# Moving the key and value projection behind a step's transposes in a paged-attention kernel

## The chip, the cores and the metric

The kernel runs on one core of a Trainium2 chip. TensorE multiplies and transposes, VectorE and ScalarE read its results out of PSUM, GpSimd does some elementwise work and issues the gathers, SyncE issues the other transfers. The metric is the device time of one execution in microseconds; the median of three runs of the kernel before is 1195.59 us (1194.82 to 1195.92).

## The reference, cut to what matters

Two layers with residual connections. The first is attention with 32 query heads, 8 key and value heads, 8 sequences of 128 tokens and a cache of 512 keys per sequence, gathered by pages:

```python
q, k, v = x @ Wq.T, x @ Wk.T, x @ Wv.T          # x: (8, 128, 512); 32, 8 and 8 heads of 128
q, k = rope(rmsnorm(q) * wq), rope(rmsnorm(k) * wk)
k_all, v_all = concat(cache[block_table], new)   # 512 cached keys and 128 new ones
p = softmax(where(valid, q @ k_all.T / sqrt(128), -1e30))
x = x + (p @ v_all) @ Wo.T
```

The second layer adds a 512x512 product and two of eight low-rank experts per token, chosen by logits. All is float32.

## The kernel before

The attention is cut into 64 groups: one key head (with its four query heads) and one sequence each. Float32 products are made of three matmuls each: every operand is split into a high part (a copy rounded to the fast format, made by ScalarE) and a low part (the rest, by subtraction on VectorE), and hi*hi, hi*lo and lo*hi are added up in PSUM (`three_passes`, lines 280 to 282). Helper `low` on line 664 does all of the subtractions, so many of VectorE's rows have that line.

One step `s` of a software pipeline, for s from -2 to 64, works on four groups at once: the attention of group s, the output product of group s-1, the transposes of queries and keys of group g1 = s+1, and the projections of group g2 = s+2. Each engine has its own function `step` and goes through its instructions strictly in that written order; semaphores join the engines. There is no planner.

TensorE's order in a step is: scores of heads 0 and 1 (line 1011), the output O of s-1, scores 2, transposes T0 of head 0's probabilities (line 1034), the query projection Q, scores 3, T1, the output projection Y, T2, the queries' transpose QT (line 1102, four 128x128 pieces), the cached keys' transpose KTC (line 1019, four), the key and value projection KV (12 matmuls, lines 280 to 282), the new keys' transpose KTN (line 1113, one), T3, and the transposes TN of the new keys' probabilities (line 1119, four). Then the next step's scores.

Scores have two PSUM buffers of their own (`ps_s`). All of the other results share four PSUM banks (`ps_w`) in turn, by their place in a fixed list:

```python
UNITS = ["O", "T0", "Q", "T1", "Y", "T2", "QT", "KTC", "KV", "KTN", "T3", "TN"]
```

A unit's bank is its place modulo 4, and `wait_bank` waits for the engine that last read the unit four places ahead. KTN waits for VectorE's split of T2, T3 for that of the queries (QT), TN for that of the cached keys (KTC), KV for the addition of Y, and the next step's O for ScalarE's copy of KV. The scores of the next step wait for the splits of queries, cached keys and new keys.

ScalarE goes through: copy and square of the projected keys and values at the start of a step, exponentials and normalisations of the heads, copies of T0 to T2, QT and KTC, then pieces of the next head's weights (`w_split`, `wo_split`), then KTN, T3 and TN. VectorE follows with the low parts in the order T2, QT, KTC, KTN, T3, TN; its `rowmax` (line 727) opens a step. In the steps -1 to 4 both split one more block of x at the end (`split_x`). In steps 62 and 63 there is no projection left; in some of its places four 128x128 pieces of the first layer's result y are transposed (`turn_x`, line 965). SyncE's `fetch_x` waits for KV and loads x again for four steps on.

Of the kernel before, what the change touches and what calls it, by code (L numbers as in the profile page):

```python
# [13 lines left out]
ACT = mybir.ActivationFunctionType  # L14
# [4 lines left out]
S = 128  # L19
# [6 lines left out]
L = PSIZE * NPP  # L26
KEYS = L + S
# [66 lines left out]
def attention_lora(nc, xT, x, wqkv, wo, kv, normw, kpos, consts, ints, w1, wB, out):  # L94
    with ExitStack() as ctx:
        def sb(name, shape, dt=F32):
            return ctx.enter_context(nc.sbuf_tensor(name, shape, dt))

        def sem(name):
            return ctx.enter_context(nc.semaphore(name))  # L100
# [24 lines left out]
        kt_hi, kt_lo = sb("kt_hi", [P, KEYS], F32R), sb("kt_lo", [P, KEYS], F32R)  # L125
# [77 lines left out]
        pe_q, pe_kv, pe_qt, pe_ktc, pe_ktn = sem("pe_q"), sem("pe_kv"), sem("pe_qt"), sem("pe_ktc"), sem("pe_ktn")  # L203
# [7 lines left out]
        a_qt, a_ktc, a_ktn, a_pt, a_norm, a_o = sem("a_qt"), sem("a_ktc"), sem("a_ktn"), sem("a_pt"), sem("a_norm"), sem("a_o")  # L211
# [18 lines left out]
        def has(g):  # L230

            return 0 <= g < G

        def wait(eng, s, g, per=1, nth=None):

            count = g * per + (per if nth is None else nth)
            if g >= 0:
                eng.wait_ge(s, count)

        def wait_kv(eng, g):  # L240

            eng.wait_ge(s_kv[g % 2], 64 * (g // 2 + 1))

        def bank(unit):
            return ps_w[:, UNITS.index(unit) % NBANK, :]
# [212 lines left out]
        def _(act):  # L458
# [62 lines left out]
            def step(s):  # L521
                g1, g2 = s + 1, s + 2

                def exps(h):

                    wait(act, d_max, s, 4, h + 1)
                    nc.scalar.activation(ps[:, h, :], ps[:, h, :], ACT.Exp, bias=negmax[:, s % 2, h:h + 1], scale=-1.0,  # L527
                                         accum_out=rowsum[:, s % 2, h:h + 1]).then_inc(a_exp, 1)

                def norm(h):  # L530

                    wait(act, d_recip, s, 4, h + 1)
                    nc.scalar.activation(ps[:, h, :], ps[:, h, :], ACT.Copy, scale=recip[:, s % 2, h:h + 1]).then_inc(a_norm, 1)  # L533

                def probs(h):

                    wait(act, pe_t, s, 4, h + 1)
                    nc.scalar.activation(pt_hi[:, 0:CT, h, :], bank(f"T{h}").rearrange("p (t q) -> p t q", t=CT),  # L538
                                         ACT.Copy).then_inc(a_pt, 1)

                def cached_keys():
                    wait(act, pe_ktc, g1)
                    nc.scalar.activation(kt_hi[:, 0:L], bank("KTC"), ACT.Copy).then_inc(a_ktc, 1)

                if has(g1):
                    wait(act, pe_kv, g1)
                    wait(act, p_v, g1 - 2, 2)
                    nc.scalar.activation(raw[:, g1 % 2, QW:WW], bank("KV")[:, 0:2 * D], ACT.Copy).then_inc(a_kv, 1)
                    wait(act, a_kv, g1)
                    wait(act, a_q, g1)  # L550
                    wait(act, d_m2, g1 - 1)
                    wait(act, p_m1, g1 - 1)
                    if s == -1:
                        act.wait_ge(d_wlo, KC)
                    nc.scalar.activation(u[:].rearrange("p h d -> p (h d)"), raw[:, g1 % 2, 0:QW + D], ACT.Square).then_inc(a_sq, 1)
                if s == -1:
                    sines()
                if has(s):
                    exps(0)
                    norm(0)  # L560
                    exps(1)
                    norm(1)
                if s == G:
                    expert_products(0)
                if has(s - 1):
                    wait(act, pe_o, s - 1)
                    wait(act, pe_y, s - 2)
                    nc.scalar.activation(o_hi[:], bank("O"), ACT.Copy).then_inc(a_o, 1)
                if s == G:

                    act.wait_ge(pe_s, 4 * G)
                    expert_products(1)
                    expert_products(2)
                if has(s):
                    probs(0)

                    wait_kv(act, s)
                    wait(act, a_kv, s)
                    wait(act, pe_o, s - 1)
                    nc.scalar.activation(v_hi[:, 0:CT, :], kv_raw[:, s % 2, :, D:2 * D], ACT.Copy).then_inc(a_vhi, 1)  # L580
                    nc.scalar.activation(v_hi[:, CT, :], raw[:, s % 2, QW + D:WW], ACT.Copy).then_inc(a_vhi, 1)
                    exps(2)
                    norm(2)
                if has(g2):
                    wait(act, pe_q, g2)
                    wait(act, d_u, g2 - 2)
                    if g2 == 1:
                        act.wait_ge(d_mask, B)
                    nc.scalar.activation(raw[:, g2 % 2, 0:QW], bank("Q"), ACT.Copy).then_inc(a_q, 1)
                turn_x(s, "Q")  # L590
                if has(s):
                    probs(1)
                    exps(3)
                    norm(3)
                    probs(2)
                if s == -1:
                    cached_keys()
                if has(g1):
                    wait(act, pe_qt, g1)
                    nc.scalar.activation(qt_hi[:], bank("QT"), ACT.Copy).then_inc(a_qt, 1)  # L600
                    if s != -1:
                        cached_keys()
                for n in W_AT.get(s, ()):
                    w_split(n)
                for n in WO_AT.get(s, ()):
                    wo_split(n)
                if has(g1):
                    wait(act, pe_ktn, g1)
                    nc.scalar.activation(kt_hi[:, L:KEYS], bank("KTN")[:, 0:S], ACT.Copy).then_inc(a_ktn, 1)
                for unit in ("QT", "KTC", "KV", "KTN"):  # L610
                    turn_x(s, unit)
                if has(s):
                    probs(3)
                    wait(act, pe_tn, s)
                    nc.scalar.activation(pt_hi[:, CT, :, :].rearrange("p h q -> p (h q)"), bank("TN"), ACT.Copy).then_inc(a_pt, 1)
                if s < 0:
                    first_wo_split(2 * (s + 2))
                    first_wo_split(2 * (s + 2) + 1)
                if 2 <= s + 3 < B:
                    split_x(s + 3)  # L620
# [41 lines left out]
        def _(dve):  # L662
            def low(out_ap, full, hi):
                return nc.vector.tensor_tensor(out_ap, full, hi.bitcast(F32), ALU.subtract)  # L664
# [52 lines left out]
            def step(s):  # L717
                g1, b = s + 1, s % B
# [93 lines left out]
                if has(g1):  # L812
# [3 lines left out]
                        cached_keys()  # L816
                    wait(dve, a_ktn, g1)
                    low(kt_lo[:, L:KEYS], bank("KTN")[:, 0:S], kt_hi[:, L:KEYS]).then_inc(d_ktn, 1)
                for unit in ("QT", "KTC", "KV", "KTN"):
                    turn_x(s, unit)  # L820
                if has(s):
                    probs(3)
                    wait(dve, a_pt, s, 5)
                    low(pt_lo[:, CT, :, :].rearrange("p h q -> p (h q)"), bank("TN"),
                        pt_hi[:, CT, :, :].rearrange("p h q -> p (h q)")).then_inc(d_pt, 1)
                if s < 0:
                    first_wo_split(2 * (s + 2))
                    first_wo_split(2 * (s + 2) + 1)
# [127 lines left out]
        def _(pe):  # L956
            def turn_x(s, unit):

                c = turned(s, unit)
                if c is None:  # L960
                    return
                wait(pe, d_y, G - B + c)
                wait_bank(pe, s, unit)
                for k in range(KC):
                    last = nc.tensor.transpose(bank(unit)[:, k * S:(k + 1) * S], y[:, c, k * P:(k + 1) * P], ident)
                last.then_inc(pe_xt, 1)
# [30 lines left out]
            def step(s):  # L997
                g1, g2 = s + 1, s + 2
# [106 lines left out]
                        turn_cached_keys()  # L1105
                turn_x(s, "QT")
                turn_x(s, "KTC")
                if has(g2) and s != -1:
                    project_keys_values()
                turn_x(s, "KV")  # L1110
                if has(g1):
                    wait_bank(pe, s, "KTN")
                    nc.tensor.transpose(bank("KTN")[:, 0:S], rot[:, REP, :], ident).then_inc(pe_ktn, 1)
# [1 line left out]
                if has(s):  # L1115
                    turn_probs(3)
                    wait_bank(pe, s, "TN")
                    for h in range(REP):
                        last = nc.tensor.transpose(bank("TN")[:, h * S:(h + 1) * S], ps[:, h, L:KEYS], ident)  # L1119
                    last.then_inc(pe_tn, 1)  # L1120

            for s in range(-2, G + 1):
                if s == -1:
# [97 lines left out]
```

## Time and profile before

| | |
|---|---|
| median of three runs | 1195.59 us |
| profiled execution | 1195.48 us |
| its span | 1193.7 us |
| TensorE matmul busy | 1155.7 us |
| TensorE weight load busy | 1025.5 us |
| ScalarE busy | 938.9 us |
| VectorE busy | 928.4 us |
| GpSimd busy | 768.2 us |

The span runs from the first to the last instruction. Busy times of TensorE are those of pipelined instructions whose ends are modelled, so the starts of its weight loads are the surest marks of where it stands. A wait that is put down to "issue" has no releaser that the profile names.

### The profile page before, as it was taken

To read this page: it belongs to the slowest core of one execution; us is meant where nothing else is said; L and a number is where in the kernel's file an instruction comes from. 1 tells how busy PE (TensorE), PEld (TensorE's weight loads), DVE (VectorE), ACT (ScalarE), POOL (GpSimd) and SP (SyncE) were. 2 spreads that over 40 slices of the span, in tenths; PEclk is the share of its full clock that TensorE was granted. 3 is DMA by queue.
4 is the path that set the end of the run, shared out by engine and by line. 5 is a ranking of instruction groups with operands and counts; after the bars stand their busy time and mean duration, and the time that the engine had idled before them with its cause. 6 is when DMAs were issued, how large, how long until landed. Compare 5 with 4: busy or idle time off the path is not lost.

```text
span 1193.7 us, 20774 instructions
## 1 busy us (share of the span) xinstructions
PE 1155.7 (97%) x6912; PEld 1025.5 (86%) x6912; DVE 928.4 (78%) x1880; ACT 938.9 (79%) x1830; POOL 768.2 (64%) x838
## 2 busy tenths in 40 slices
PE   3799999999999999999999999999999999999998
PEld 2688888888888888888888888888888888888787
DVE  6788887787878777887877787778878777877746
ACT  3787888888888888888888888888888888888741
POOL 5566666667677667676776766667667667666500
PEclk9899999999999999999999999999999999999999
DMA  6322412221222122122213222231222122121001
GB/s 237 119 85 96 146 61 80 94 93 48 93 94 76 64 93 94 53 88 93 90 51 94 93 67 74 93 94 49 92 93 81 58 92 91 55 69 54 18 1 71
DMA packets 53626, 98.11 MB, mean 82 GB/s; under 512 B 8592, under 2 KB 25872, under 8 KB 53264
## 3 DMA queue, kind: packets, MB, share of 16 engines
q1 hardware_dynamic: 41232, 63.21, 15.1%
q0 software_dynamic: 12288, 33.57, 9.5%
q8 instruction: 57, 0.93, 0.3%
q14 instruction: 49, 0.40, 0.1%
HBM read 90.45 MB, written 6.29 MB: 81 GB/s over the span
## 4 chain that ended last, share of the span: by engine, by line
PE 85%; DVE 5%; ACT 5%; issue 3%; DMA 1%; SPq 1%; POOL 0%; DVEq 0%; POOLq 0%; ACTq 0%
PE ps_s L1011 18%; PE ps_w L282 16%; PE ps_w L281 16%; PE ps_w L280 16%; PE ps_w L1034 8%; PE ps_w L1119 2%; PE ps_w L1102 2%; PE ps_s L993 2%; PE ps_w L1019 2%; ACT ps L527 2%; DVE pt_lo L664 2%; ACT ps L533 1%; DVE ps L727 1%; DMA y<-wo 1%; ACT pt_hi L538 1%
## 5 line engine op out<-in xcount | busy, mean ns | idle before, releaser
L406 POOL DMA_INDIRECT kv_raw<-kv,rows x256 | 254.0, 992 | 93.8 <-issue 62.7
L527 ACT ACTIVATE ps<-ps,negmax 128x640 f32<-128x640 f32 x256 | 211.9, 828 | 82.9 <-DVE negmax L727 49.4
L533 ACT ACTIVATE ps<-ps,recip 128x640 f32<-128x640 f32 x256 | 212.9, 832 | 71.0 <-DVE recip L734 52.9
L664 DVE TENSOR_TENSOR pt_lo<-ps_w,pt_hi 128x512 fp32r<-128x512 f32 x322 | 210.0, 684 | 58.5 <-ACT pt_hi L538 57.2
L727 DVE CUSTOM_DVE_ANT_0 ps<-ps_s,mask 128x640 f32<-128x640 f32 x256 | 206.6, 815 | 13.3 <-PE ps_s L1011 13.3
L280 PE MATMUL ps_w<-w_hi,xt_hi 128*128 128x512 f32 (+1 forms) x512 | 183.7, 359 | 11.5 <-DVE w_lo L664 8.2
L538 ACT ACTIVATE pt_hi<-ps_w 128x512 fp32r<-128x512 f32 x256 | 152.6, 596 | 27.8 <-PE ps_w L1034 21.5
L282 PE MATMUL ps_w<-w_hi,xt_lo 128*128 128x512 f32 (+1 forms) x512 | 173.2, 338 | 0.0
L281 PE MATMUL ps_w<-w_lo,xt_hi 128*128 128x512 f32 (+1 forms) x512 | 173.0, 338 | 0.0
L427 POOL TENSOR_TENSOR rot<-u,cos 128x640 f32<-128x640 f32 x64 | 101.8, 1591 | 110.0 <-DVE u L783 110.0
L1034 PE MATMUL ps_w<-cst,ps 128*128 128x128 f32 x1024 | 153.9, 273 | 7.1 <-DVE pt_lo L664 4.7
L434 POOL TENSOR_TENSOR rot<-rot,m 128x320 f32<-128x320 f32 x128 | 110.4, 884 | 51.3 <-DVE m L790 51.1
L1034 PEld LDWEIGHTS ps_w<-cst,ps 128*128 128x128 f32 x1024 | 124.5, 141 | 19.4 <-issue 10.4
L790 DVE TENSOR_TENSOR m<-u,sin 128x640 f32<-128x640 f32 x64 | 125.3, 1957 | 0.3 <-issue 0.3
L282 PE MATMUL ps_w<-pt_hi,v_lo 128*128 128x512 f32 x320 | 125.2, 391 | 0.0
L281 PE MATMUL ps_w<-pt_lo,v_hi 128*128 128x512 f32 x320 | 125.1, 391 | 0.0
L1011 PE MATMUL ps_s<-kt_hi,qt_hi 128*128 128x320 f32 x512 | 121.9, 319 | 3.2 <-DVE kt_lo L664 2.2
L280 PE MATMUL ps_w<-pt_hi,v_hi 128*128 128x512 f32 x320 | 124.9, 390 | 0.0
L1011 PE MATMUL ps_s<-kt_hi,qt_lo 128*128 128x320 f32 x512 | 117.5, 311 | 0.0
L1011 PE MATMUL ps_s<-kt_lo,qt_hi 128*128 128x320 f32 x512 | 117.4, 310 | 0.0
L280 PEld LDWEIGHTS ps_w<-w_hi,xt_hi 128*128 128x128 f32 x512 | 97.2, 190 | 20.8 <-DVE xt_lo L664 8.2
L1011 PEld LDWEIGHTS ps_s<-kt_hi,qt_hi 128*128 128x128 f32 x512 | 89.0, 189 | 25.3 <-issue 13.4
(155 smaller groups left out, 2583.1 us busy)
## 6 DMA issues: line engine op xcount, KB each, us to landing
xt_hi<-xsplit SPq DMA_DIRECT2D x56, 256.0 KB
xt_lo<-xsplit SPq DMA_DIRECT2D x56, 256.0 KB
w_raw<-wqkv SPq DMA_DIRECT2D x56, 192.0 KB
wo_raw<-wo SPq DMA_DIRECT2D x56, 128.0 KB
kv_raw<-kv,rows POOLq DMA_INDIRECT x256
xsplit<-xt_hi SPq DMA_DIRECT2D x8, 256.0 KB
xsplit<-xt_lo SPq DMA_DIRECT2D x8, 256.0 KB
y<-x SPq DMA_DIRECT2D x2, 1024.0 KB, 7.2
```

The costliest lines, as they stand in the source:

```text
L280: nc.tensor.matmul(out_ap, a_hi, b_hi, start=start and k == 0, stop=False)
L281: nc.tensor.matmul(out_ap, a_hi, b_lo, start=False, stop=False)
L282: last = nc.tensor.matmul(out_ap, a_lo, b_hi, start=False, stop=stop and k == n - 1)
L406: pool.indirect_dma_start(kv_raw[:, g % 2, t, :], None, kv[:, :], bass.IndirectOffsetOnAxis(rows[:, g % B, t:t + 1], 0)).then_inc(s_kv[g % ...
L527: nc.scalar.activation(ps[:, h, :], ps[:, h, :], ACT.Exp, bias=negmax[:, s % 2, h:h + 1], scale=-1.0, accum_out=rowsum[:, s % 2, h:h + 1]) ...
L533: nc.scalar.activation(ps[:, h, :], ps[:, h, :], ACT.Copy, scale=recip[:, s % 2, h:h + 1]).then_inc(a_norm, 1)
L538: nc.scalar.activation(pt_hi[:, 0:CT, h, :], bank(f"T{h}").rearrange("p (t q) -> p t q", t=CT), ACT.Copy).then_inc(a_pt, 1)
L664: return nc.vector.tensor_tensor(out_ap, full, hi.bitcast(F32), ALU.subtract)
L727: nc.vector.tensor_tensor_reduce(out=halves(ps[:, h, :]), in0=ps_s[:, h % 2, :, 0:KH], in1=halves(mask[:, b, :]), scale=-SCALE, scalar=3.0 ...
L790: nc.vector.tensor_tensor(m2[:], u[:], sin[:, g1 % B, :].unsqueeze(1).to_broadcast([P, NH, D]), ALU.mult).then_inc(d_m2, 1)
L1011: last = nc.tensor.matmul(ps_s[:, h % 2, half, 0:KH], a, c[:, half * KH:(half + 1) * KH], start=n == 0, stop=n == 2)
L1034: last = nc.tensor.transpose(bank(f"T{h}")[:, t * S:(t + 1) * S], ps[:, h, t * P:(t + 1) * P], ident)
```

## The change

On TensorE the projection KV of steps 0 to 61 leaves its place between KTC and KTN and goes behind TN, directly ahead of the next step's scores. KTN follows KTC. In steps -2 and -1 nothing changes. On ScalarE the copy of KTN goes ahead of `w_split` and `wo_split`. The transposes of y in KV's unit (steps 62 and 63) move behind TN on all three engines. The list `UNITS`, and with it the banks and what each unit waits for, stays as it is.

```diff
 # scalar engine, step(s)
+                if has(g1):
+                    wait(act, pe_ktn, g1)
+                    nc.scalar.activation(kt_hi[:, L:KEYS], bank("KTN")[:, 0:S], ACT.Copy).then_inc(a_ktn, 1)
                 for n in W_AT.get(s, ()):
                     w_split(n)
                 for n in WO_AT.get(s, ()):
                     wo_split(n)
-                if has(g1):
-                    wait(act, pe_ktn, g1)
-                    nc.scalar.activation(kt_hi[:, L:KEYS], bank("KTN")[:, 0:S], ACT.Copy).then_inc(a_ktn, 1)
-                for unit in ("QT", "KTC", "KV", "KTN"):
+                for unit in ("QT", "KTC", "KTN"):
                     turn_x(s, unit)
                 if has(s):
                     probs(3)
...
+                turn_x(s, "KV")
 # vector engine, step(s)
-                for unit in ("QT", "KTC", "KV", "KTN"):
+                for unit in ("QT", "KTC", "KTN"):
                     turn_x(s, unit)
...
+                turn_x(s, "KV")
 # tensor engine, step(s)
                 turn_x(s, "QT")
                 turn_x(s, "KTC")
-                if has(g2) and s != -1:
+                if s == -2:
                     project_keys_values()
-                turn_x(s, "KV")
                 if has(g1):
                     wait_bank(pe, s, "KTN")
                     nc.tensor.transpose(bank("KTN")[:, 0:S], rot[:, REP, :], ident).then_inc(pe_ktn, 1)
...
                     last.then_inc(pe_tn, 1)
+                if has(g2) and s >= 0:
+                    project_keys_values()
+                turn_x(s, "KV")
```

## Rows read from the trace of the kernel before

**Rows 1.** The page, section 1: busy us, share of the span, instructions.

```profile
PE 1155.7 (97%) x6912; PEld 1025.5 (86%) x6912; DVE 928.4 (78%) x1880; ACT 938.9 (79%) x1830; POOL 768.2 (64%) x838
```

**Rows 2.** Waits: engine, line, releaser: us in total, times, longest us.

```profile
PEld ps_s L1011 <- issue: 13.4, 57, 0.5
...
PE ps_w L1102 <- POOL rot L434: 9.1, 1, 9.1
...
SPq L334 <- PE ps_w L282: 850.1, 55, 16.0
```

**Rows 3.** Timeline, TensorE's weight loads, step 26: start us, length us, instruction.

```profile
502.05 0.59 PEld L1034 LDWEIGHTS ps_w<-cst,ps 128*128 128x128 f32 x4
...
503.48 0.19 PEld L280 LDWEIGHTS ps_w<-w_hi,xt_hi 128*128 128x128 f32 x1
...
504.92 0.14 PEld L1113 LDWEIGHTS ps_w<-cst,rot 128*128 128x128 f32 x1
505.03 0.47 PEld L1034 LDWEIGHTS ps_w<-cst,ps 128*128 128x128 f32 x4
505.49 0.44 PEld L1119 LDWEIGHTS ps_w<-cst,ps 128*128 128x128 f32 x4
506.16 0.30 PEld L1011 LDWEIGHTS ps_s<-kt_hi,qt_hi 128*128 128x128 f32 x2 [0.23 <-issue]
```

**Rows 4.** Timeline, VectorE, end of step 26 and start of 27.

```profile
503.55 0.69 DVE L664 TENSOR_TENSOR pt_lo<-ps_w,pt_hi 128x512 fp32r<-128x512 f32 x1 [0.37 <-ACT pt_hi L538]
504.16 0.68 DVE L664 TENSOR_TENSOR qt_lo<-ps_w,qt_hi 128x512 fp32r<-128x512 f32 x1
504.76 0.68 DVE L664 TENSOR_TENSOR kt_lo<-ps_w,kt_hi 128x512 fp32r<-128x512 f32 x1
505.64 0.29 DVE L664 TENSOR_TENSOR kt_lo<-ps_w,kt_hi 128x128 fp32r<-128x128 f32 x1 [0.21 <-ACT kt_hi L609]
...
507.60 0.81 DVE L727 CUSTOM_DVE_ANT_0 ps<-ps_s,mask 128x640 f32<-128x640 f32 x1
```

**Rows 5.** Timeline, ScalarE, end of step 26 and start of 27.

```profile
502.92 0.60 ACT L538 ACTIVATE pt_hi<-ps_w 128x512 fp32r<-128x512 f32 x1
...
506.74 0.39 ACT L548 ACTIVATE raw<-ps_w 128x256 f32<-128x256 f32 x1
```

**Rows 6.** Timeline, TensorE's matmuls, T2 of step 26.

```profile
502.28 0.60 PE L1034 MATMUL ps_w<-cst,ps 128*128 128x128 f32 x4
```

**Rows 7.** Timeline, VectorE and then TensorE's weight loads, step 62.

```profile
1128.46 0.88 DVE L664 TENSOR_TENSOR kt_lo<-ps_w,kt_hi 128x512 fp32r<-128x512 f32 x2
...
1125.33 0.42 PEld L1102 LDWEIGHTS ps_w<-cst,rot 128*128 128x128 f32 x4 [0.17 <-POOL rot L434]
...
1129.20 0.42 PEld L1119 LDWEIGHTS ps_w<-cst,ps 128*128 128x128 f32 x4
1129.58 0.30 PEld L1011 LDWEIGHTS ps_s<-kt_hi,qt_hi 128*128 128x128 f32 x2
```

**Rows 8.** Timeline, early steps and step 62's first scores: weight loads, last VectorE.

```profile
51.26 0.42 PEld L1119 LDWEIGHTS ps_w<-cst,ps 128*128 128x128 f32 x4
52.20 0.30 PEld L1011 LDWEIGHTS ps_s<-kt_hi,qt_hi 128*128 128x128 f32 x2 [0.52 <-issue]
...
65.93 0.42 PEld L1034 LDWEIGHTS ps_w<-cst,ps 128*128 128x128 f32 x4 [0.56 <-issue]
...
159.93 0.30 PEld L1011 LDWEIGHTS ps_s<-kt_hi,qt_hi 128*128 128x128 f32 x2 [0.23 <-issue]
...
1112.07 0.30 PEld L1011 LDWEIGHTS ps_s<-kt_hi,qt_hi 128*128 128x128 f32 x2 [0.23 <-issue]
...
71.80 0.68 DVE L664 TENSOR_TENSOR xt_lo<-y,xt_hi 128x512 fp32r<-128x512 f32 x1
```

**Rows 9.** Windows: stretch, length, busy us by engine (instructions), granted TensorE clock, DMA.

```profile
34.60:39.00 4.40, 4.34 (x16) 4.37 (x17) 3.31 (x8) 2.65 (x6) 0.00 (x0) 0.50 0.41 131
...
1140.70:1145.50 4.80, 3.81 (x28) 2.78 (x27) 3.62 (x7) 4.01 (x9) 0.00 (x0) 1.00 0.00 0
```

## The prediction, written before the result was known

> **What bounds the kernel now.** I first read the page's busy shares: TensorE's matmuls cover 97% of the span [rows 1]. The reader should see that an engine this full can only get slower by being made to wait, and can only get faster by the few waits it has. So next comes the view of waits. Its largest regular entry on TensorE is 13.4 us in 57 places, 0.235 us each, in front of the first score matmuls of a step [rows 2]. Everything else there is a start-up wait. Then I read one ordinary step, step 26, instruction by instruction on four engines, because a change of order is priced where the order is.
>
> In step 26 the weight loads run: third probability transposes (T2) at 502.05, query transposes, cached-key transposes, KV projection from 503.48, new-key transpose (KTN) at 504.92, fourth probability transposes (T3) at 505.03, last-tile transposes (TN) at 505.49, and the next scores at 506.16 [rows 3]. There is no hole up to TN, and one of 0.23 us before the scores. What releases the scores is in VectorE's rows: the low part of the new keys starts at 505.64 and takes 0.29, so it ends at 505.93, and the load stands 0.23 behind it [rows 4]. The hole is therefore the wait for the new keys' split.
>
> The second reading is less visible and matters more. TN writes the bank that held the cached keys' transpose, and has to wait until VectorE has read it: kt_lo starts at 504.76 and takes 0.68, ending at 505.44; TN's load starts at 505.49, 0.05 behind [rows 3, 4]. The two columns agree in this way in each of the 51 steps where both rows stand by themselves. So TN is already at its earliest moment: VectorE's chain and TensorE's chain arrive together, and what lets TensorE arrive so late is the KV projection in front of it. VectorE's chain itself starts from TensorE: T2 ends at 502.88 (502.28 + 0.60) [rows 6], ScalarE copies it at 502.92 [rows 5], VectorE takes it at 503.55, then the queries at 504.16, then the cached keys at 504.76 [rows 4]. That is three PSUM reads in a row at 0.60 spacing, and the diff does not touch their order.
>
> **The change, part by part.**
> *Moved on TensorE: the KV projection (12 weight loads and 12 matmuls) from before KTN to behind TN.* Its length is 504.92 - 503.48 = 1.44 us [rows 3]. It was the cover under which three banks were emptied. Without it KTN, T3 and TN each arrive early and wait: KTN needs pt_lo of T2, ending at 503.55 + 0.69 = 504.24; T3 needs qt_lo, ending at 504.16 + 0.68 = 504.84; TN needs kt_lo, ending at 505.44 [rows 4]. With 0.05 to 0.11 behind each, TN's load stands again at 505.49. So the projection's whole 1.44 comes behind an unmoved TN: TN's four loads take 0.44, the projection 1.44, and the next scores start 1.88 behind TN's start, rounded down to 1.87 for the 0.43 seen between groups. Before it was 506.16 - 505.49 = 0.67.
>
> *Removed: the 0.23 wait for the new keys.* KTN moves from 504.92 to about 504.29, and its copy goes ahead of the weight splits on ScalarE, so its kt_lo comes right behind that of the cached keys, near 505.65. The scores now come near 507.36, 1.7 later, so that wait goes. It is contained in the 0.67. What is late next is TensorE itself. The sum per step is 1.87 - 0.67 = **+1.20 us**.
>
> *ScalarE: the new-key copy ahead of w_split and wo_split.* Those two now wait for KTN, ending near 504.6; their results are used by VectorE in the next step and by TensorE much later. They end near 505.6, when T3 is just done, so nothing queues. Price 0; if T3's copy were held by 0.3, VectorE's rowmax of the next step would still have more room than before (next point).
>
> *New neighbour: KV directly ahead of scores, and its copy at the head of the next ScalarE step.* ScalarE's copy of KV stood at 506.74, 0.58 behind the scores' start [rows 5]; it will stand about 0.2 behind it. The attention output's bank waits for this copy, but comes after two score groups. Queued behind it are the square and the exponentials, which wait for rowmax(0). That began 507.60 - 506.16 = 1.44 behind the scores, because VectorE was still busy with T3's and TN's splits [rows 3, 4]. Those splits now end before scores(0) does, so rowmax(0) starts when scores(0) is done, an estimated 1.1 behind. ScalarE and VectorE thus enter a step about 0.3 earlier relative to TensorE. It buys nothing in an ordinary step, as T2's copy starts 0.04 behind TensorE already.
>
> *SyncE's queue:* the fetch of x for four steps on waits for this same projection, as it does now (55 waits [rows 2]); it and the weight loads queued behind it are issued nearly 2 us later and used more than a step, 17 us, later. Price 0. GpSimd waits for the cached keys' transpose, which does not move.
>
> **Where the 1.20 does not hold.** Steps 1 to 6 are slower now: the scores' first load goes from 52.20 to 159.93, 107.73 us for six steps, 17.96 each, against (1112.07 - 159.93)/55 = 17.31 later [rows 8]. They carry an extra x split on ScalarE and VectorE between TN's split and rowmax(0) (71.80 on VectorE), and T2 then waits 0.56 for the late chain (65.93) [rows 8]. The new order gives VectorE about 1.9 us before the scores need it, so this split fits there and the wait goes. I take these steps at the new ordinary period, 17.31 + 1.20 = 18.51: 6 x 18.51 - 107.73 = +3.3. Step 0 has TN at 51.26 and scores at 52.20 [rows 8]: 1.87 - 0.94 = +0.93. The 55 steps 7 to 61 give 55 x 1.20 = +66.0. In steps 62 and 63 no projection is left, but the transposes of y in its unit move behind TN, 0.44 each: +0.9. **Sum:** 0.9 + 3.3 + 66.0 + 0.9 = +71.1.
>
> Step 62 is the control in the same trace, for there the projection is missing already. T3 and TN stall as I say they will: kt_lo begins at 1128.46, the first of its two parts ends 0.68 later at 1129.14, TN's load is at 1129.20, and the scores follow at 1129.58, without the hole [rows 7]. It also shows the unknown, what a drained TensorE queue costs: between two groups behind a stall there is a hole of 0.17 (1125.33), between TN and the scores none [rows 7]. So the cost of restarting is bounded by 0 and 0.17 per step, 0 to 10.5 us in 62 steps; I take 0, from the row of the same place. From below: T2's copy waits 0.04 for TensorE or for ScalarE's own queue, and in some steps ScalarE is up to 0.1 late, which the earlier chain could give back: 0 to -6 us.
>
> The profiled execution took 1195.48 us for a span of 1193.7, 0.1 below the median of 1195.59, so no correction: 1195.5 + 71.1 = **1266.6 us**.
>
> **The clock.** In the new order about 3.4 us of a step hold transposes and waits alone. In this trace 4.80 us of just that (1140.70 to 1145.50) ran at a granted clock of 1.00, the 2.4 GHz level, while the only stretch at 0.50, the 1.2 GHz level, followed 9.1 us of idleness in the start-up [rows 2, 9]. The Trainium skill, TensorE: Matmul & The Clock Gate, Part 4 (PE-mode transpose), says that transposes do not count as activity for the clock gate, which speaks against bunching them. By that rule the case is the rival B below; in this trace the row just quoted goes against it.
>
> **The rivals.**
> A. *Faster.* The waits for the banks could be no real limit, TN following KTN and T3 at once, and only the removed hole would count: 62 x -0.23 = -14, 1181 us. For it: the hole is the one regular wait on the full engine. Against it: the 0.05 between kt_lo and TN, and step 62. It decides only if VectorE's three reads ended 1.2 us earlier, and nothing in the diff shortens them. 2%.
> B. *Clock.* TensorE at 0.50 when the projection starts: 1.44 more per step, 62 x 1.44 = +89, 1356 us. 2%.
> C. *Restart cost.* Each of three released groups pays 0.17 and one at the scores is exposed, or two: 0.2 to 0.4 per step, +12 to +25 on top, 1279 to 1291 us. 9%.
> D. *The other engines give some back.* The earlier entry of ScalarE and VectorE shortens the chain T2 to kt_lo by 0.3 per step: -19, 1248 us. Against it: the chain starts from T2's end on TensorE. 7%.
>
> **Numbers.** The forecast has 80%: 1266.6, own range 1256 (-6 from below, -3 should the early steps recover more) to 1277 (+10.5). Toward C and D I stretch a little, 1254 to 1280. Faster by over 0.2% (about what a measurement of this kernel tells from no change) comes only from A, 2%; within 0.2% I give 1%; slower 97%.
>
> **What would show it.** After: kt_lo of the cached keys still 3.16 behind T2's start and TN's load 0.05 behind it; three small idle times on TensorE before KTN, T3 and TN, about 1.4 us a step together, released by VectorE's pt_lo, qt_lo and kt_lo; no "issue" hole before the scores; a period of 18.5 us; early steps equal to late ones. A TN whose load stands less than 3.1 us behind T2's start would prove the bank argument wrong; a hole before the KV projection or the scores would mean C; granted clocks below 1.00 after step 1 would mean B.

## The result and the profile after

The changed kernel takes 1266.66 us (median of 4 runs, 1264.8 to 1267.16) against 1195.64 us of the kernel before (4 runs). The ratio is 1.0591, with a 95% interval of 1.0577 to 1.0605: slower by 5.9%. The span of the profiled execution grew from 1193.7 to 1265.4 us, by 71.7.

The page's section 1, and the waits of TensorE (engine, line, releaser: us in total, times, longest us), of the changed kernel:

```profile
PE 1174.8 (93%) x6912; PEld 1028.3 (81%) x6912; DVE 929.4 (73%) x1880; ACT 946.3 (75%) x1830; POOL 767.9 (61%) x838
...
PE ps_w L1114 <- DVE pt_lo L665: 36.5, 63, 1.4
PE ps_w L1036 <- DVE qt_lo L665: 22.5, 63, 0.4
```

Line numbers from TensorE's part on are a little higher than before: KTN is L1114, T3 L1036, TN L1120, the scores L1013, VectorE's split L665. The instruction counts are those of [rows 1]. What is new is two waits in each of 63 steps: KTN for T2's split, T3 for the queries'. The 57 holes before the scores of [rows 2] are gone from the list. Matmul busy time rose by 19 us although the same 6912 ran: the record of a released-late instruction no longer overlaps the one ahead of it, and can be longer (KTN's transpose is 0.33 us on average, before 0.27), so this column is no measure of added work.

One ordinary step, step 26, in the timeline of the changed kernel (start us, length us): weight loads, then VectorE.

```profile
531.42 0.59 PEld L1036 LDWEIGHTS ps_w<-cst,ps 128*128 128x128 f32 x4
...
532.42 0.47 PEld L1021 LDWEIGHTS ps_w<-cst,kv_raw 128*128 128x128 f32 x4
533.66 0.14 PEld L1114 LDWEIGHTS ps_w<-cst,rot 128*128 128x128 f32 x1 [0.78 <-DVE pt_lo L665]
534.32 0.42 PEld L1036 LDWEIGHTS ps_w<-cst,ps 128*128 128x128 f32 x4 [0.52 <-issue]
534.86 0.42 PEld L1120 LDWEIGHTS ps_w<-cst,ps 128*128 128x128 f32 x4
535.25 0.19 PEld L280 LDWEIGHTS ps_w<-w_hi,xt_hi 128*128 128x128 f32 x1
...
536.67 0.31 PEld L1013 LDWEIGHTS ps_s<-kt_hi,qt_hi 128*128 128x128 f32 x2
...
532.92 0.69 DVE L665 TENSOR_TENSOR pt_lo<-ps_w,pt_hi 128x512 fp32r<-128x512 f32 x1 [0.38 <-ACT pt_hi L538]
533.52 0.68 DVE L665 TENSOR_TENSOR qt_lo<-ps_w,qt_hi 128x512 fp32r<-128x512 f32 x1
534.12 0.88 DVE L665 TENSOR_TENSOR kt_lo<-ps_w,kt_hi 128x512 fp32r<-128x512 f32 x2
535.65 1.29 DVE L665 TENSOR_TENSOR pt_lo<-ps_w,pt_hi 128x512 fp32r<-128x512 f32 x2 [0.65 <-ACT pt_hi L538]
537.87 0.82 DVE L728 CUSTOM_DVE_ANT_0 ps<-ps_s,mask 128x640 f32<-128x640 f32 x1 [0.94 <-PE ps_s L1013]
```

Read it against [rows 3, 4]. From T2's first load to TN's first load it takes 534.86 - 531.42 = 3.44 us; before, 505.49 - 502.05 = 3.44. TN has not moved by a hundredth. Each load stands just behind the VectorE instruction that empties its bank: KTN at 533.66 behind 532.92 + 0.69 = 533.61, T3 at 534.32 behind 533.52 + 0.68 = 534.20, TN at 534.86 behind 534.12 + 0.68 = 534.80 (the row of 534.12 holds two splits; the first, of the cached keys, takes 0.68 as in [rows 4]). The projection of 1.42 us (535.25 to 536.67) now stands alone behind TN. No wait of TensorE ends under it: the scores' inputs are ready before it begins, and the split of TN, which the next O needs, ends at 535.65 + 1.29 = 536.94, 1.47 ahead of O's load at 538.41.

The first score loads of steps 1, 7 and 62, to be set beside [rows 8], in the same view:

```profile
55.09 0.41 PEld L1013 LDWEIGHTS ps_s<-kt_hi,qt_hi 128*128 128x128 f32 x2
...
167.38 0.19 PEld L1013 LDWEIGHTS ps_s<-kt_hi,qt_hi 128*128 128x128 f32 x1
...
1182.97 0.31 PEld L1013 LDWEIGHTS ps_s<-kt_hi,qt_hi 128*128 128x128 f32 x2
```

The ordinary period is (1182.97 - 167.38)/55 = 18.465 us, against 17.31.

### The profile page after: what moved, and what is told of

It is laid out like the page before. It is cut to its first block, busy times and chain, and to the rows that moved or that the text cites. A ratio compares the mean times of both kernels' runs of the same rounds, so it can differ in the third digit from the quotient of the medians.

```text
span 1265.4 us, 20774 instructions
## 1 busy us (share of the span) xinstructions
PE 1174.8 (93%) x6912; PEld 1028.3 (81%) x6912; DVE 929.4 (73%) x1880; ACT 946.3 (75%) x1830; POOL 767.9 (61%) x838
## 4 chain that ended last, share of the span: by engine, by line
PE 80%; DVE 10%; ACT 5%; issue 3%; DMA 1%; SPq 0%; POOL 0%; DVEq 0%; POOLq 0%
PE ps_s L1013 17%; PE ps_w L282 16%; PE ps_w L281 16%; PE ps_w L280 16%; PE ps_w L1036 9%; DVE pt_lo L665 4%; ACT pt_hi L538 3%; DVE qt_lo L665 3%; PE ps_w L1120 3%; PE ps_s L995 2%; ACT ps L527 1%; DMA y<-wo 1%; ACT ps L533 1%; DVE ps L728 1%; DVE w_lo L665 0%
## 5 line engine op out<-in xcount | busy, mean ns | idle before, releaser
L665 DVE TENSOR_TENSOR pt_lo<-ps_w,pt_hi 128x512 fp32r<-128x512 f32 x322 | 210.0, 683 | 70.2 <-ACT pt_hi L538 68.8
L728 DVE CUSTOM_DVE_ANT_0 ps<-ps_s,mask 128x640 f32<-128x640 f32 x256 | 209.4, 818 | 59.4 <-PE ps_s L1013 56.5
L280 PE MATMUL ps_w<-w_hi,xt_hi 128*128 128x512 f32 (+1 forms) x512 | 185.0, 361 | 10.8 <-DVE w_lo L665 8.3
L1036 PE MATMUL ps_w<-cst,ps 128*128 128x128 f32 x1024 | 155.9, 275 | 27.2 <-DVE qt_lo L665 22.5
L1036 PEld LDWEIGHTS ps_w<-cst,ps 128*128 128x128 f32 x1024 | 122.7, 141 | 47.5 <-issue 37.3
L280 PE MATMUL ps_w<-pt_hi,v_hi 128*128 128x512 f32 x320 | 125.2, 391 | 0.0
L791 DVE TENSOR_TENSOR m<-u,sin 128x640 f32<-128x640 f32 x64 | 120.1, 1877 | 0.3 <-issue 0.3
L1013 PE MATMUL ps_s<-kt_hi,qt_hi 128*128 128x320 f32 x512 | 117.2, 310 | 1.5 <-DVE kt_lo L665 1.5
L1013 PE MATMUL ps_s<-kt_hi,qt_lo 128*128 128x320 f32 x512 | 117.3, 310 | 0.0
L1013 PE MATMUL ps_s<-kt_lo,qt_hi 128*128 128x320 f32 x512 | 117.2, 310 | 0.0
L280 PEld LDWEIGHTS ps_w<-w_hi,xt_hi 128*128 128x128 f32 x512 | 98.7, 193 | 20.4 <-DVE xt_lo L665 8.2
L735 DVE RECIPROCAL recip<-rowsum 128x1 f32<-128x1 f32 x256 | 40.9, 160 | 93.3 <-ACT ps L527 86.4
```

Source lines behind the costliest of these rows:

```text
L280: nc.tensor.matmul(out_ap, a_hi, b_hi, start=start and k == 0, stop=False)
L728: nc.vector.tensor_tensor_reduce(out=halves(ps[:, h, :]), in0=ps_s[:, h % 2, :, 0:KH], in1=halves(mask[:, b, :]), scale=-SCALE, scalar=3.0 ...
L791: nc.vector.tensor_tensor(m2[:], u[:], sin[:, g1 % B, :].unsqueeze(1).to_broadcast([P, NH, D]), ALU.mult).then_inc(d_m2, 1)
L1013: last = nc.tensor.matmul(ps_s[:, h % 2, half, 0:KH], a, c[:, half * KH:(half + 1) * KH], start=n == 0, stop=n == 2)
L1036: last = nc.tensor.transpose(bank(f"T{h}")[:, t * S:(t + 1) * S], ps[:, h, t * P:(t + 1) * P], ident)
```

## The experiments

All kernels were timed in three rounds beside the kernel before, but for the two repeats at the end. The ordinary period is read from the timeline of each.

| kernel | median us | ratio to before (95%) | ordinary period us |
|---|---|---|---|
| before | 1195.6 to 1196.2 | 1 | 17.31 |
| changed | 1266.66 | 1.0591 (1.0577 to 1.0605) | 18.47 |
| TensorE part alone | 1265.36 | 1.0587 (1.0570 to 1.0605) | 18.47 |
| ScalarE part alone | 1211.59 | 1.0132 (1.0115 to 1.0149) | 17.57 |
| KV between KTN and T3 | 1239.19 | 1.0361 (1.0344 to 1.0378) | 17.94 |
| KV between T3 and TN | 1263.37 | 1.0564 (1.0547 to 1.0582) | 18.37 |
| changed, shorter chain | 1252.37 | 1.0471 (1.0453 to 1.0488) | 18.25 |
| before, shorter chain | 1195.33 | 0.9997 (0.9987 to 1.0006) | 17.31 |
| KTN inside KV, ScalarE as changed | 1191.99 | 0.9969 (0.9957 to 0.9982) | 17.22 |
| KTN inside KV, ScalarE as before | 1186.17 | 0.9922 (0.9906 to 0.9939) | 17.14 |

**The TensorE part alone.** The changed kernel with ScalarE's three blocks in their old order:

```diff
-                if has(g1):
-                    wait(act, pe_ktn, g1)
-                    nc.scalar.activation(kt_hi[:, L:KEYS], bank("KTN")[:, 0:S], ACT.Copy).then_inc(a_ktn, 1)
                 for n in W_AT.get(s, ()):
                     w_split(n)
                 for n in WO_AT.get(s, ()):
                     wo_split(n)
+                if has(g1):
+                    wait(act, pe_ktn, g1)
+                    nc.scalar.activation(kt_hi[:, L:KEYS], bank("KTN")[:, 0:S], ACT.Copy).then_inc(a_ktn, 1)
```

> The diff's TensorE part alone: ScalarE keeps the copy of the new keys behind the weight splits. Theory (VectorE's three reads T2, queries, cached keys set TN, and the projection comes whole behind it): the scores are 1.8 us behind TN, so a copy 0.9 us later is still early; same as the changed kernel, 1266.7 +- 2. Rival (the new keys' split is what the scores wait for, and the ScalarE move hides it): a hole before the scores of 0.2 or more a step, 1279 or above.

Measured: 1265.36, the same period. The whole loss is in TensorE's order; the ScalarE edit gives nothing here.

**The ScalarE part alone.** The kernel before with the copy of KTN ahead of the splits:

```diff
+                if has(g1):
+                    wait(act, pe_ktn, g1)
+                    nc.scalar.activation(kt_hi[:, L:KEYS], bank("KTN")[:, 0:S], ACT.Copy).then_inc(a_ktn, 1)
                 for n in W_AT.get(s, ()):
                     w_split(n)
                 for n in WO_AT.get(s, ()):
                     wo_split(n)
-                if has(g1):
-                    wait(act, pe_ktn, g1)
-                    nc.scalar.activation(kt_hi[:, L:KEYS], bank("KTN")[:, 0:S], ACT.Copy).then_inc(a_ktn, 1)
```

> The diff's ScalarE part alone, KV stays ahead of KTN. Theory: KTN is done at the same time as before, so the new keys' copy starts no earlier; ScalarE stands idle for it, and the two weight splits come 0.4 to 0.5 us later and push T3's and TN's copies, rowmax(0) and in the end T2's copy, which has 0.04 us of room: slower, some 0.4 us a step, 1220 (1205 to 1232). Rival (the ScalarE move removes the 0.23 us hole): 1181.

Measured: 1211.59, slower by 1.3%, inside the expected range but by another path. The timeline of a step of this kernel (ScalarE, VectorE, weight loads):

```profile
530.61 0.28 ACT L605 ACTIVATE kt_hi<-ps_w 128x128 fp32r<-128x128 f32 x1 [0.78 <-PE ps_w L1113]
530.78 0.52 ACT L478 ACTIVATE w_hi<-w_raw 128x384 fp32r<-128x384 f32 x1
...
532.12 1.29 DVE L664 TENSOR_TENSOR pt_lo<-ps_w,pt_hi 128x512 fp32r<-128x512 f32 x2 [0.91 <-ACT pt_hi L538]
...
531.43 0.30 PEld L1011 LDWEIGHTS ps_s<-kt_hi,qt_hi 128*128 128x128 f32 x2 [0.19 <-issue]
...
533.46 0.19 PEld L280 LDWEIGHTS ps_w<-pt_hi,v_hi 128*128 128x128 f32 x1 [0.27 <-DVE pt_lo L664]
```

ScalarE idles 0.78 us for KTN, as expected, and the copies of T3 and TN come late. But what stops TensorE is neither T2's copy nor TN: it is the output product O of the next step (L280 at 533.46), which needs the split of TN (532.12 + 1.29 = 533.41). That 0.27 us is the loss of a step (17.57 - 17.31 = 0.26). From step 59 on, when `wo_split` has ended, the period of this kernel is 17.31: with nothing pushed behind the copy, the edit costs nothing. This is a third limit that I had priced at zero in the kernel before: there O's load is at 507.88, in the timeline of the kernel before,

```profile
507.88 0.19 PEld L280 LDWEIGHTS ps_w<-pt_hi,v_hi 128*128 128x128 f32 x1
```

and the split of TN ended by about 507.7, 0.2 us ahead of it.

**KV between KTN and T3; KV between T3 and TN.** Two steps of the projection's way back (both edits in one listing, with its comments added here):

```diff
                 turn_x(s, "KTN")
+                if has(g2) and s >= 0:      # first kernel
+                    project_keys_values()
                 if has(s):
                     turn_probs(3)
+                if has(g2) and s >= 0:      # second kernel, in place of the first
+                    project_keys_values()
+                if has(s):
                     wait_bank(pe, s, "TN")
...
-                if has(g2) and s >= 0:
-                    project_keys_values()
                 turn_x(s, "KV")
```

> The changed kernel, but the projection stands between KTN and T3. Theory: only KTN's wait (0.8 us, for VectorE's split of T2) stays open, the projection covers those of T3 and TN, and the hole before the scores goes: scores 0.56 us later than before, 62 x 0.56 = +35, 1230 (1226 to 1234). Rival (any order without KV ahead of KTN loses the whole projection): 1266. Rival (the transposes bunched together are the cost, by the clock or the queue): near 1196.

> The changed kernel, but the projection stands between T3 and TN. Theory: the waits of KTN (0.8 us) and T3 (0.55 us) are open, only TN's 0.1 us is covered: scores 1.06 to 1.11 us later than before, 1262 (1259 to 1265). Rival (the three waits count alike): about half way between the kernel with KV behind KTN and the changed one, 1248.

Measured: the second as expected (1263.37; the period grew by 1.06). The first is 1239.19, 9 us above the forecast of 1230, outside its range. Its timeline (weight loads, VectorE):

```profile
541.65 0.14 PEld L1114 LDWEIGHTS ps_w<-cst,rot 128*128 128x128 f32 x1 [0.84 <-DVE pt_lo L665]
...
544.02 0.30 PEld L1013 LDWEIGHTS ps_s<-kt_hi,qt_hi 128*128 128x128 f32 x2
...
545.86 0.19 PEld L280 LDWEIGHTS ps_w<-pt_hi,v_hi 128*128 128x128 f32 x1
...
544.52 1.29 DVE L665 TENSOR_TENSOR pt_lo<-ps_w,pt_hi 128x512 fp32r<-128x512 f32 x2 [1.53 <-ACT pt_hi L538]
```

The one open wait at KTN is there (0.84), and from the queries' first load the scores stand at 4.07 to 4.11 against 506.16 - 502.61 = 3.55 before, so 0.52 to 0.56 as forecast. The rest of an ordinary step is again O: 545.86 - 544.02 = 1.84 behind the scores, against 1.72 before, right behind the split of TN (544.52 + 1.29 = 545.81). With the projection ahead of T3, the transposes T3 and TN stand close to the scores and their splits end too late for O. So the period grew by 0.63 and not by 0.56, which is 4 of the 9 us. Of the others some 2 lie in steps 1 to 6, where the scores' first loads are 113.36 us apart and not 107.73: KTN waits 1.4 us there. About 1 is in step 0, which ran partly at half clock (0.79 granted over 44 to 60 us), of which more below. The last 2 are behind the scores of step 62, where the granted clock was 0.50 from 1170.9 to 1174.3 us; why it fell there stays open. The rival by which any order without KV ahead of KTN loses all of it is dead. So are that of bunched transposes as the whole cost (near 1196), and, by the second kernel, that of three waits that count alike (1248): what counts is which waits the projection lies in front of.

**A shorter chain, in both kernels.** VectorE's split of the queries covers a quarter of the columns from step 1 on; the other three quarters of the low part keep old values.

```diff
-                    low(qt_lo[:], bank("QT"), qt_hi[:]).then_inc(d_qt, 1)
+                    qc = slice(0, QW if s < 1 else S)
+                    low(qt_lo[:, qc], bank("QT")[:, qc], qt_hi[:, qc]).then_inc(d_qt, 1)
```

> The changed kernel with VectorE's split of the queries cut to the first 128 of 512 columns from step 1 on (the rest of the low part keeps old values). Theory: this shortens the chain T2, queries, cached keys by about 0.4 us, so TN's load stands 2.8 instead of 3.2 us behind T2's start and the step is 0.4 us shorter: 1266.7 - 24 = 1242 (1239 to 1246). Rival (the loss is in TensorE itself, from bunched transposes or the projection beside the scores): 1266 unchanged.

> The kernel before with the same cut of the queries' split. Theory: VectorE's chain and TensorE arrive at TN together, so a shorter chain gives TensorE at most 0.05 us a step, and the hole before the scores, which hangs on KTN, stays: 1195.6, at best 1193. Rival (VectorE's chain bounds the kernel before as well): 1171, 0.4 us a step.

Measured: the changed kernel gains 14 us, 1252.37; the kernel before gains nothing, 0.9997 with an interval across 1. So VectorE's chain bounds the one and not the other, which is the heart of the theory. The timeline of the kernel before with the cut (weight loads, VectorE) shows it in a step:

```profile
500.77 0.59 PEld L1035 LDWEIGHTS ps_w<-cst,ps 128*128 128x128 f32 x4
...
504.18 0.47 PEld L1120 LDWEIGHTS ps_w<-cst,ps 128*128 128x128 f32 x4
504.88 0.30 PEld L1012 LDWEIGHTS ps_s<-kt_hi,qt_hi 128*128 128x128 f32 x2 [0.23 <-issue]
...
503.25 0.69 DVE L664 TENSOR_TENSOR kt_lo<-ps_w,kt_hi 128x512 fp32r<-128x512 f32 x1
```

The bank of TN is free 0.24 us ahead of its load (503.25 + 0.69 = 503.94), yet TN stands 3.41 behind T2 and not 3.44, and the scores 4.11 behind T2 as before: with the projection in front, TensorE has nothing to gain from the shorter chain.

In the changed kernel the size was wrong, 0.22 us a step and not 0.4, and the time outside the expected range. Its timeline with the cut (ScalarE, VectorE, weight loads):

```profile
544.23 0.60 ACT L543 ACTIVATE kt_hi<-ps_w 128x512 fp32r<-128x512 f32 x1
...
544.50 0.28 DVE L665 TENSOR_TENSOR qt_lo<-ps_w,qt_hi 128x128 fp32r<-128x128 f32 x1
544.87 0.89 DVE L665 TENSOR_TENSOR kt_lo<-ps_w,kt_hi 128x512 fp32r<-128x512 f32 x2
...
545.61 0.42 PEld L1121 LDWEIGHTS ps_w<-cst,ps 128*128 128x128 f32 x4 [0.30 <-DVE kt_lo L665]
```

VectorE's split of the queries ends at 544.78, but kt_lo starts at 544.87, behind ScalarE's copy of the same keys (544.23 + 0.60 = 544.83). ScalarE's three copies are the next chain behind VectorE's three splits, 0.2 us shorter. TN still follows kt_lo by 0.05.

**KTN inside the projection.** The kernel before with its projection in two parts, 9 matmuls, then KTN, then 3 matmuls; once with ScalarE's order of the change and once with the old one.

```diff
-                if has(g2) and s != -1:
+                parts = has(g2) and s >= 0
+                if s == -2:
                     project_keys_values()
+                if parts:
+                    wait_bank(pe, s, "KV")
+                    project_part(0, 3)
                 turn_x(s, "KV")
                 if has(g1):
                     wait_bank(pe, s, "KTN")
                     nc.tensor.transpose(bank("KTN")[:, 0:S], rot[:, REP, :], ident).then_inc(pe_ktn, 1)
+                if parts:
+                    project_part(3, KC)
```

> The kernel before with KTN's one transpose put inside the projection, behind 9 of its 12 matmuls, and the new keys' copy ahead of the weight splits on ScalarE. Theory: KTN is 0.36 us earlier and still behind T2's split, ScalarE reaches it at once, so the 0.23 us hole before the scores goes while TN stays where it is: 57 x -0.23 = -13, 1182.5 (1180 to 1187). Rival (the hole is issue time of four waits in a row on TensorE, which no order removes): 1195.6.

> The same with ScalarE's order of before (new keys' copy behind the weight splits). Theory: ScalarE comes to the copy when the two splits are done, 0.1 to 0.15 us earlier than before, so about half of the hole goes: 1188 (1184 to 1192). Rival (ScalarE's place does not matter): as with the ScalarE move, 1182.

Measured: both gain, so the hole before the scores was the wait for the new keys' split and no issue time. But the order of the two is the reverse of what I wrote: with ScalarE's old order it is 1186.17 (0.9922), inside its range, with the new one 1191.99 (0.9969), above its range. The timeline of the better one (weight loads, VectorE):

```profile
501.18 0.14 PEld L1124 LDWEIGHTS ps_w<-cst,rot 128*128 128x128 f32 x1
...
502.16 0.42 PEld L1132 LDWEIGHTS ps_w<-cst,ps 128*128 128x128 f32 x4
502.60 0.30 PEld L1011 LDWEIGHTS ps_s<-kt_hi,qt_hi 128*128 128x128 f32 x2
...
504.36 0.19 PEld L280 LDWEIGHTS ps_w<-pt_hi,v_hi 128*128 128x128 f32 x1
...
501.42 0.95 DVE L664 TENSOR_TENSOR kt_lo<-ps_w,kt_hi 128x512 fp32r<-128x512 f32 x2
503.01 1.29 DVE L664 TENSOR_TENSOR pt_lo<-ps_w,pt_hi 128x512 fp32r<-128x512 f32 x2 [0.64 <-ACT pt_hi L538]
```

The scores follow TN after 0.44 us and not after 0.67: the whole hole of 0.23 is gone, with the old order too. There the new keys' split follows that of the cached keys at once (the row of 501.42 holds both and ends at 502.37, 0.23 ahead of the scores), where in [rows 4] it waited 0.21 for ScalarE. Of the 0.23 us, 0.04 goes back at O, now 1.76 behind the scores and right behind the split of TN (503.01 + 1.29 = 504.30). The period falls by 0.17 on the average of 55 steps. With ScalarE's new order O waits longer, 4.1 us in 20 places by the view of waits, and the period falls by 0.09 only. The kernel with the old order beats the kernel before by 0.8% and the changed one by 6.4% (1186.17 to 1266.66).

**The clock of step 0.** The first profile of the changed kernel has a stretch at half clock. Windows view (stretch, length, busy us and instructions by engine, granted clock):

```profile
48.80:55.80 7.00, 6.16 (x30) 5.50 (x29) 4.07 (x7) 5.01 (x12) 5.43 (x7) 0.53 0.21 56
```

So two kernels were profiled again, with no edit.

> The changed kernel once more, for one look at step 0, where its first profile shows a granted clock of 0.50 from about 48.8 to 55.8 us. If the lower clock is a property of this order of work (transposes without the projection between them), it is there again and KV's scores stand 3.4 us behind TN in step 0. If it depends on how the execution falls, it may be 1.00 and 1.8 us; the execution is then some 3 us shorter, 1264.

> The diff's TensorE part alone once more, whose first profile shows a clock of 1.00 in step 0 with the same order on TensorE. If the order of transposes decides the clock, the two repeats agree with each other; if it is chance, either level can show in either kernel. 1264 at 1.00, 1267 at 0.50.

Windows of the same stretch, of the changed kernel's repeat and of the repeat of the TensorE part alone:

```profile
44.00:60.00 16.00, 12.66 (x66) 11.19 (x65) 10.78 (x21) 11.84 (x24) 10.16 (x12) 0.79 0.36 116
```

```profile
44.00:60.00 16.00, 11.87 (x79) 10.53 (x78) 12.29 (x25) 13.24 (x27) 11.20 (x13) 1.00 0.35 107
```

Each kernel shows again what it showed the first time: 0.79 and 0.79, 1.00 and 1.00. Their TensorE orders are equal, so the order of the transposes does not decide it; the ScalarE part alone, with TensorE's old order, shows 0.89 in this stretch. Nor can the work of ScalarE's edit be the cause: the clock has fallen by 48 to 49 us, and the first copy that the edit moves runs at 50.4 or 50.8.

The fall goes with a difference that stands already in the start-up. Windows, of the changed kernel and of the TensorE part alone:

```profile
21.30:22.20 0.90, 0.90 (x6) 0.90 (x6) 0.70 (x2) 0.90 (x3) 0.00 (x0) 0.50 0.84 306
```

```profile
21.30:22.20 0.90, 0.71 (x7) 0.47 (x5) 0.90 (x3) 0.88 (x2) 0.46 (x2) 1.00 0.77 275
```

Of the twelve profiles, six have 0.50 there, and just these six fall again in step 0: both of the changed kernel, ScalarE alone, KV between KTN and T3, the changed kernel with the shorter chain, KTN inside KV with ScalarE's new order. The other six have 1.00 in both places. At 22 us all of these kernels still go through the same instructions. What decides it stays open: six of the seven profiles with ScalarE's new order show the fall and none of the five with the old one, while single runs of one kernel differ too (mean granted clock of the four runs of the TensorE part alone: 0.991 to 0.994; of the changed kernel: 0.989 to 0.992).

The price of the fall in these profiles is known: in step 0 the scores' load stands 3.42 us behind TN's where other steps have 1.81, so 1.6 us from there on; the spans are 1265.4 and 1265.2 us against 1262.5 and 1264.4.

## Why the prediction was right, point by point

It was right in sign, mechanism and size: 1266.6 forecast, 1266.66 measured. The exactness is partly luck, for the terms of the sum were off by small amounts that cancelled. Measured at the scores' first loads of both profiles:

| term | forecast | measured |
|---|---|---|
| step 0 | +0.93 | 55.09 - 52.20 = +2.9 |
| steps 1 to 6 | +3.3 | 112.29 - 107.73 = +4.6 |
| steps 7 to 61 | +66.0 | 1015.59 - 952.14 = +63.5 |
| steps 62, 63 and the tail | +0.9 | +0.8 |
| sum | +71.1 | +71.7 |

- **TN is set by VectorE's third read and does not move.** Shown: 3.44 from T2 in both traces, and 14 us gained in one kernel and none in the other by shortening that chain. That chain is ScalarE's copies and VectorE's splits together: with one split shorter, the copies bound it after 0.22 us.
- **The projection comes whole behind it.** Shown, with a size a little too large: TN to scores is 1.81 and not 1.87, for TN's four loads take 0.39 and not 0.44 and the projection 1.42 and not 1.44. The period grew by 1.155 and not by 1.20, and 55 x 0.045 is the 2.5 us missing in the third row.
- **The hole before the scores goes.** Shown, and its cause by the kernel with KTN inside the projection.
- **Three small waits, about 1.4 us together.** Shown: 0.78, 0.52 and about 0.1 of idle weight loads.
- **ScalarE's move costs nothing.** Right in the changed kernel, where the scores are so late that O has room. It would have been wrong in any order with TN close to the scores; the ScalarE part alone shows 0.26 us a step. I had named O's wait for KV's copy and not its wait for the split of TN.
- **Early steps at the ordinary period.** Half right. The x split is hidden now, as forecast. But in every second one VectorE also splits two pieces of weights, T2's split is late, and KTN's load idles 1.25 us in place of 0.78: 19.03, 18.92 and 18.95 us for steps 1, 3 and 5, about 18.46 for the others. Nor were all small waits of [rows 2] start-up waits: in the kernel before, T3's load waits some 0.5 us in each of the steps 0 to 5.
- **Step 0.** Off by 2 us, of which 1.6 is the half clock told above. Rival B, which I priced for all 62 steps, happened in one. The rule on which it rested (the Trainium skill, TensorE: Matmul & The Clock Gate, Part 4) did not decide the ordinary steps: each of them holds 3.8 us of transposes and waits alone (531.42 to 535.25 in step 26), and the windows view gives a granted clock of 1.00 over 60 to 1260 us.
- **Restart cost (rival C) and give-back (rival D).** The 0.17 of [rows 7], taken as what a restart costs, is put down by its row to GpSimd's `rot`, so it was no measure of that. Neither rival came true: no hole before the projection or the scores, and rowmax(0) starts 537.87 - 536.67 = 1.2 us behind the scores in place of 1.44 without shortening T2 to kt_lo.

## What to carry to other kernels

Where an engine is nearly full, ask of each piece of work what waits it covers, not what it costs. The same 1.4 us of projection covered three bank waits from in front of them; behind the first of them a step was 0.63 us longer, behind the second 1.06, behind the third 1.16. Put the cover ahead of the first of several waits that follow each other, and pull out of it the small instruction on whose result the next phase depends (here one transpose: -0.8%). An instruction moved ahead of others in a strict queue is only earlier if its input is there; otherwise those behind it pay.

## What the runs showed of the hardware that was not expected

The distance from a VectorE end to the TensorE load that it releases differs by place: 0.05 us at KTN and TN (533.61 to 533.66, 534.80 to 534.86), 0.12 at T3 (534.20 to 534.32), and 0.23 at the scores of the kernel before (505.93 to 506.16). The number of waits that follow in the code does not explain it: one more follows the blocking wait at the scores, but two more follow it at O, whose load in the ScalarE part alone stands 0.05 behind (533.41 to 533.46). The reason is open.

A stall of 2.6 to 2.8 us in step 0 stands in all twelve profiles, ahead of T2. The granted clock fell to 0.50 within 1 us of its end in six of them and stayed at 1.00 in the other six; the same six had been at 0.50 at 21.3 to 22.2 us as well. The cause is open.
